# SwitchHead: the small products for the maxima half a turn later, in a turn of scores, value projection, output projection, values

## The reference, cut to what matters

```python
def _moe_attn(x, Wq, Wk, Wv, Wo, Wsel_v, Wsel_o):      # 16 heads of 64, 8 experts, the best 2 kept
    q = _rope(jnp.einsum('bsd,hdp->bhsp', x, Wq))
    k = _rope(jnp.einsum('bsd,hdp->bhsp', x, Wk))
    gv = _gate(x, Wsel_v)
    v = jnp.einsum('bsd,bhse,hedp->bhsp', x, gv, Wv)
    att = jax.nn.softmax(jnp.einsum('bhsp,bhtp->bhst', q, k) / np.sqrt(P), axis=-1)
    o = jnp.einsum('bhst,bhtp->bhsp', att, v)
    go = _gate(x, Wsel_o)
    return jnp.einsum('bhsp,bhse,hepd->bsd', o, go, Wo)
```

## Time and profile before

| | before |
|---|---|
| median of 3 runs | 5247.22 us (5242.2 to 5261.81) |
| the profiled execution's own time | 5249.07 us |
| its span, first to last instruction | 5247.3 us |
| mean granted TensorE clock | 0.956 |
| busy: TensorE, vector engine, ScalarE, GpSimd | 86%, 76%, 63%, 56% of the span |

### The profile page before, as it was taken

One profiled execution on the slowest core, in us unless ns is written; L12 is line 12 of the kernel. 1 busy time (PEld: TensorE's weight loads), 2 busy tenths in 40 slices (PEclk: granted clock), 3 DMA queues, 4 the chain that ended last, 5 costly groups with the idle time before them and its releaser, 6 DMA issues.

```text
span 5247.3 us, 113107 instructions
## 1 busy us (share of the span) xinstructions
PE 4487.2 (86%) x42666; PEld 2217.8 (42%) x42666; DVE 3972.3 (76%) x4717; ACT 3322.4 (63%) x7061; POOL 2912.4 (56%) x2205
## 2 busy tenths in 40 slices
PE   6999998668999999998999888996898888888856
PEld 2333433334555555555555445553333322222226
DVE  5989898768877786778877886776777688888721
ACT  5666565347677777776767666772555557667743
POOL 4888888757867776767767656763212222120014
PEclk8999999889999999999999999998999999999978
DMA  4555555413343343333333332333111111011005
GB/s 149 188 185 181 181 187 189 152 46 97 97 106 93 93 108 88 95 98 89 108 85 92 89 102 74 91 106 72 44 37 31 42 35 23 20 31 20 2 32 170
DMA packets 258831, 488.61 MB, mean 93 GB/s; under 512 B 58731, under 2 KB 108398, under 8 KB 257636
## 3 DMA queue, kind: packets, MB, share of 16 engines
q1 hardware_dynamic: 255288, 475.05, 32.3%
q0 software_dynamic: 3008, 6.32, 0.3%
HBM read 435.33 MB, written 35.30 MB: 90 GB/s over the span
## 4 chain that ended last, share of the span: by engine, by line
PE 65%; issue 13%; DVE 9%; ACT 8%; POOL 5%; DMA 0%; SPq 0%; POOLq 0%; DVEq 0%; ACTq 0%
PE ps L2347 8%; PE ps L1450 8%; PE ps L1440 8%; PE ps L1398 7%; PE ps L1412 7%; PE ps L548 4%; PE ps L2318 4%; PE ps L2300 3%; ACT n_P L2382 3%; PE ps L495 2%; PE ps L1391 2%; DVE ps L713 1%; DVE n_MX L2461 1%; DVE m_HH L734 1%; DVE m_HH L728 1%
## 5 line engine op out<-in xcount | busy, mean ns | idle before, releaser
L2461 DVE TENSOR_REDUCE n_MX<-ps 128x2 f32<-128x1024 f32 (+6 forms) x1034 | 982.4, 979 | 235.8 <-PE ps L2300 134.8
L2382 ACT ACTIVATE n_P<-ps 128x1024 f32<-128x1024 f32 (+4 forms) x1022 | 825.2, 838 | 447.1 <-PE ps L2318 233.5
L1570 ACT ACTIVATE s_P<-s_P,s_MB 128x256 f32<-128x256 f32 x2048 | 1009.5, 501 | 0.3
L1724 DVE TENSOR_REDUCE s_MX<-s_P 128x4 f32<-128x1024 f32 x512 | 599.7, 1213 | 307.8 <-ACT s_P L1555 307.8
L1555 ACT ACTIVATE s_P<-ps 128x1024 f32<-128x1024 f32 x512 | 495.9, 1021 | 380.0 <-PE ps L1412 379.8
L771 POOL TENSOR_TENSOR m_PR<-m_HH,m_CS 128x1024 f32<-128x1024 f32 x256 | 606.0, 2382 | 156.6 <-issue 129.2
L1971 POOL TENSOR_TENSOR XTB<-XTB 128x512 f32<-128x512 f32 x256 | 331.8, 1296 | 586.8 <-DVE XTB L1715 586.8
L1741 DVE STREAM_TRANSPOSE shared<-s_P 128x1024 f32<-128x1024 f32 x512 | 603.2, 1207 | 23.2 <-ACT s_P L1570 23.2
L1952 POOL TENSOR_TENSOR s_OG<-s_OG,s_OT 128x1024 f32<-128x1024 f32 x256 | 606.9, 2372 | 23.7 <-DMA s_OG<-s_gt 23.7
L1450 PE MATMUL ps<-s_OG,s_WO 128*128 128x512 f32 x1024 | 511.9, 623 | 33.6 <-POOL s_OG L1952 23.7
L1412 PE MATMUL ps<-s_QF 64*32 64x256 f32 x16384 | 508.3, 383 | 29.8 <-POOL s_QF L1944 20.0
(11 more groups left out here) (359 smaller groups left out, 6818.4 us busy)
## 6 DMA issues: line engine op xcount, KB each, us to landing
m_CS<-m_rows_c SPq DMA_DIRECT2D x256, 512.0 KB, 3.8
s_OG<-s_gt SPq DMA_DIRECT2D x512, 256.0 KB, 4.2
m_BS<-m_rows_c SPq DMA_DIRECT2D x80, 512.0 KB
s_WV<-in_s_v SPq DMA_DIRECT2D x32, 512.0 KB, 4.0
s_TA<-XTB SPq DMA_DIRECT2D x256, 64.0 KB, 2.3
s_OR<-s_sums SPq DMA_DIRECT2D x128, 128.0 KB, 3.8
s_WO<-in_s_o SPq DMA_DIRECT2D x32, 512.0 KB, 5.3
g_WB<-in_g_wx SPq DMA_DIRECT2D x23, 578.0 KB, 4.3
```

What stands on the lines that cost most here:

```text
L1570: ins = s.activation(P, P, ACT.Exp, bias=self.MB[:, g % 2, 4 * h + a:4 * h + a + 1], accum_out=self.SU[:, g // 4 % 2, at:at + 1])
L2382: ins = s.activation(P[:, at:at + x.shape[1], lo:512], x[:, :, lo:512], ACT.Exp, scale=scale)
L2461: ins = v.tensor_reduce(self.MX[:, q, at:at + x.shape[1], hp, t], x[:, :, 0:width], AX.X, ALU.max)
```

## The change

The join leaves the ring. The flipped maxima and the spread bias get places of their own in the values' bank: self.O shrinks from 512 to 128 columns, self.flip and self.spread lie behind it. So the bank holds one tile's values, keep copies each tile by itself (four copies of 128 columns in place of one of 512), and values wait for the copy of the tile before and for the bias to have been read. In a turn the steps stand in another order: most of tile m-1 and keep of tile m-3 come with the next scores, v comes ahead of gated, onto and max, join comes behind values, and the turn's second transpose behind join.

```diff
-        self.O, self.Z = PS[:, 3072:3584], PS[:, 3584:4096]
-        ring = ("rows", "gate", "gate_t", "qk", "v", "row", "join", "f_t", "f_rows",
+        self.O, self.Z = PS[:, 3072:3200], PS[:, 3584:4096]
+        self.flip, self.spread = PS[0:32, 3200:3328], PS[:, 3328:3336]
+        ring = ("rows", "gate", "gate_t", "qk", "v", "row", "f_t", "f_rows",
...
         k, half = m % 4, lambda late: self.of_half((m - late) // 4)
+        if due(1):
+            out.insert(len(out) - due(0), ("most", *tile(1)))
+        if due(3):
+            out.insert(len(out) - due(0), ("keep", *tile(3)))
...
+        for _ in range(2 if m == 2 else 1):
+            next(vs, None)
         if due(self.GATED):
             h, e = part(self.GATED)
             out.append(("gated", *self.of_half(h), e))
...
         if due(0):
             out.append(("max", *tile(0)))
-        for _ in range(2 if m == 2 else 1):
-            next(vs, None)
-        if due(0):
-            out.append(("join", *tile(0)))
         if due(1):
             out.extend([("exp", *tile(1), 0), ("exp", *tile(1), 1)])
...
         if due(1):
-            out.extend([("turn", *tile(1), 0), ("turn", *tile(1), 1)])
+            out.append(("turn", *tile(1), 0))
...
             out.append(("values", *self.pair(g // 8), g % 8))
-            if g % 4 == 3:
-                out.append(("keep", *self.of_half(g // 4)))
         if due(0):
-            out.append(("most", *tile(0)))
+            out.append(("join", *tile(0)))
+        if due(1):
+            out.append(("turn", *tile(1), 1))
...
             elif kind == "most":
-                g, join = self.tile(*step[1:]), ("join", *step[1:])
+                g = self.tile(*step[1:])
                 pe.wait_ge(self.most_done, g + 1)
+                if g > 0:
+                    pe.wait_ge(self.bias_read, g)
...
-                if g % 4 == 0:
-                    pe.wait_ge(self.o_done, g // 4)
+                if g > 0:
+                    pe.wait_ge(self.o_done, g)
+                pe.wait_ge(self.bias_read, min(g + 2, 64 * NB))
...
             elif kind == "keep":
-                k = self.half(*step[1:])
-                s.wait_ge(self.values_done, 4 * (k + 1))
-                if k > 1:
-                    s.wait_ge(self.ot_done, k - 1)
-                s.activation(self.OR[k % 2][:, 0, :], self.O, ACT.Copy).then_inc(self.o_done, 1)
+                g = self.tile(*step[1:])
+                s.wait_ge(self.values_done, g + 1)
+                if g >= 8:
+                    s.wait_ge(self.ot_done, g // 4 - 1)
+                s.activation(self.OR[g // 4 % 2][:, 0, 128 * (g % 4):128 * (g % 4) + 128], self.O,
+                             ACT.Copy).then_inc(self.o_done, 1)
```

More of the change, by code:

```diff
@@ L898, in __init__ @@
         for name in ("consts_in", "zeroed", "ln_chain", "ln_out", "top_v", "own_top", "b2_done", "spill_out", "top_done", "gates_out", "gv_out", "raw_done", "swap_in", "turn_done",
-                     "rope_done", "wq_in", "wv_in", "gvj_in", "v_done", "mx_zero", "mx_done", "flipped", "most_done", "exp_done",
+                     "rope_done", "wq_in", "wv_in", "gvj_in", "v_done", "mx_zero", "mx_done", "flipped", "most_done", "bias_full", "bias_read", "exp_done",
                      "pt_done", "values_done", "o_done", "su_out", "su_in", "recip_done", "sums_out", "or_in", "ot_done", "og_done", "wo_in", "onto_done", "outt_done", "wf_in", "xn_in", "aff_done",
@@ L933, in order @@
             elif t == 6:
-                out.extend([("most", *self.of_tile(1)), ("turn", *self.of_tile(0), 1)])
+                out.append(("turn", *self.of_tile(0), 1))
         out.append(("gates_of", *self.pair(1)))
@@ L1419, in tensor @@
                 pe.wait_ge(self.mx_done, g + 1)
-                r.empty(pe, step)
-                pe.transpose(ps[0:32, 0:128], self.MX[:, g % 2, :], c.ident[:, :]).then_inc(self.flipped, 1)
+                pe.transpose(self.flip, self.MX[:, g % 2, :], c.ident[:, :]).then_inc(self.flipped, 1)
             elif kind == "most":
-                g, join = self.tile(*step[1:]), ("join", *step[1:])
+                g = self.tile(*step[1:])
                 pe.wait_ge(self.most_done, g + 1)
+                if g > 0:
+                    pe.wait_ge(self.bias_read, g)
                 for x in range(4):
-                    ins = pe.matmul(r.ap(join)[32 * x:32 * x + 32, 512:520], self.MR[:, g % 2, :], c.ident[:, 0:8],
+                    ins = pe.matmul(self.spread[32 * x:32 * x + 32, :], self.MR[:, g % 2, :], c.ident[:, 0:8],
                                     start=True, stop=True)
-                ins.then_inc(*r.fill(join))
+                ins.then_inc(self.bias_full, 1)
             elif kind == "values":
@@ L1433, in tensor @@
                     pe.wait_ge(self.v_done, 8 * (self.turns(b, j) + 1))
-                if g % 4 == 0:
-                    pe.wait_ge(self.o_done, g // 4)
+                if g > 0:
+                    pe.wait_ge(self.o_done, g)
+                pe.wait_ge(self.bias_read, min(g + 2, 64 * NB))
                 for i in range(NT):
                     for h in range(2):
-                        place = self.O[64 * h:64 * h + 64, 128 * (g % 4):128 * (g % 4) + 128].rearrange("p (a n) -> p a n", n=32)
+                        place = self.O[64 * h:64 * h + 64, :].rearrange("p (a n) -> p a n", n=32)
                         P = self.PT[g % 2][:, h, :].rearrange("p (a k n) -> p a k n", a=4, n=32)[:, :, i, :]
@@ L1556, in scalar @@
             elif kind == "most":
-                g, join = self.tile(*step[1:]), ("join", *step[1:])
-                r.filled(s, join)
+                g = self.tile(*step[1:])
+                s.wait_ge(self.bias_full, g + 1)
                 if g > 1:
                     s.wait_ge(self.exp_done, 2 * (g - 1))
-                s.activation(self.MB[:, g % 2, :], r.ap(join)[:, 512:520], ACT.Copy).then_inc(*r.take(join))
+                s.activation(self.MB[:, g % 2, :], self.spread, ACT.Copy).then_inc(self.bias_read, 1)
             elif kind == "exp":
@@ L1564, in scalar @@
                 if h == 0:
-                    r.taken(s, ("join", *step[1:4]))
+                    s.wait_ge(self.bias_read, g + 1)
                     if g % 4 == 0 and g >= 8:
@@ L1730, in vector @@
                 if g > 1:
-                    r.filled(v, ("join", *self.of_tile(g - 2)))
-                v.tensor_reduce(self.MR[0:8, g % 2, :], ps[0:8, 0:128].rearrange("p (x n) -> p n x", x=4), AX.X, ALU.max,
+                    v.wait_ge(self.bias_full, g - 1)
+                v.tensor_reduce(self.MR[0:8, g % 2, :], self.flip[0:8, :].rearrange("p (x n) -> p n x", x=4), AX.X, ALU.max,
                                 negate=True).then_inc(self.most_done, 1)
@@ L1978, in gpsimd @@
                 g.wait_ge(self.or_in, 32 * (k + 1))
-                g.wait_ge(self.o_done, k + 1)
+                g.wait_ge(self.o_done, 4 * (k + 1))
                 if k > 1:
```

## The result

The changed kernel takes 5324.97 us (median of 4 runs, 5319.61 to 5329.88), the kernel before 5247.35 us (4 runs): a ratio of 1.0143, 95% interval 1.0121 to 1.0166. It is slower, by 78 us.

A forecast was written before the change was run, and what follows sets the result against it. TensorE was taken to bound the stage, busy 2231.9 of 2480 us, so only its idle time could change. Terms 64 + 45 + 30 + 5 - 35 - 10 = +99 us on 5249.07 gave 5348 us, range 5275 to 5415.

The forecast's parts named there:

- what comes back: TensorE waits that shrink: flips in the last seven turns or late through ScalarE, s_OUTT, small reduce, vector pieces: -35 us.
- the slot of the key projection: The earlier value projection must wait until the vector engine has read the query or key projection's ring slot: +30 us.
- The turn m%8=1: After each eighth, v waits for values with the maxima and flip queued behind: 3.9 us gap for 1.74, 30 times, +64.
- v's own wait: Sign to look for: in turns m%8=1 the vector engine waits some 3.8 us for the values, about 115 in all.
- The clock: Each of the 30 new gaps ahead of the flip drops TensorE's clock to half and is paid twice: +45 us.
- The rival by which the gap is paid once: Rival, chance 0.15: the clock doesn't fall behind the m%8=1 gaps, so only the gaps count: 5303 us.
- The plain case: Value projection behind a query or key projection, no other work ahead of the slot's read: 0.44 us, 62 turns, 27.
- GpSimd and ScalarE: GpSimd's v steps delay its gate product, +5 us; ScalarE's four small keep copies are hidden, 0.
- vector pieces: Vector engine pieces such as L1660 stand later, about when GpSimd's gate product ends, and run faster: -10 us.
- the rival by which the pieces get out of each other's way: Rival, chance 0.09: all 90 us of TensorE idle time from vector pieces goes, not 10: 5268 us.
- The faster rival: Rival, chance 0.10: TensorE's waits ahead of small products and flip vanish, 170 us less: 5079 us.
- the sentence that the wait could not be met earlier: Against the faster case: values of m-2 can't end 3.6 us earlier for v at m%8=1, as three blocks stand ahead.

The follow-up runs named there:

- wait_off: The changed kernel without the vector engine's own wait for the values at the first v of a pair: 5193.94 us, 0.9882 of the kernel before.
- filler: The changed kernel with nine unread matmuls ahead of the flip in turns m%8=1, filling TensorE's gap: 5286.86 us, 1.0061 of the kernel before.
- v_behind: The changed kernel's late flip and small products, but v behind output projection and maxima as before: 5135.89 us, 0.9772 of the kernel before.
- v_ahead_only: The kernel before with v ahead of gate product, output projection and maxima, and no vector-engine wait for the values: 5691.91 us, ratio 1.0848.

## Why the prediction was right, point by point

The idle times make up the sum: +46.0 (flip), -52.0 (small products), +42.1 (value projection), -1.1 (output projection), +4.2 (scores, 8.2 to 12.4 us), together 39. Busy time adds the other 39: an estimate is 46 by the clock (the difference to wait_off, which has the same order), less 7 that the order saves. That is the 77 us of the turns. The forecast was 99. The mechanism held, and the 21 us too many are in the sizes of two terms: what comes back was put 33 us too small, and the slot of the key projection 12 too small.

*The turn m%8=1.* Forecast: a gap of 3.9 us in place of 1.74 by the same measure, +64 us. Measured: 3.84 us ahead of the flip where 1.68 us stood ahead of the small products, 30 times: +65. One sign came out otherwise: v's own wait was put at 3.8 us each, 115 in all, and measured some 5.1, 154.1 in all. The vector engine reaches v sooner; the gap doesn't grow by that, since v starts when the values end. Taking the wait away moved the time by what was expected, so the cause is shown.

*The clock.* Forecast +45, measured by the filler 38 net, and 45 to 46 in TensorE's busy time. The rule of the Trainium skill ("TensorE: Matmul & The Clock Gate", section "Why this matters for your kernels": idle gaps in mid-kernel bring the clock down to half) agrees: the window behind the gap has a granted clock of 0.59, the one behind the filler 1.00. The rival by which the gap is paid once fell.

*The slot of the key projection.* Forecast +30, measured +42. The plain case was 0.41 us for 0.44 forecast; 20 turns with a piece of other work ahead of L1708 waited 1.4 to 2.5 us, where I had taken 13 turns at 1 us.

*GpSimd and ScalarE.* Forecast +5 and 0; measured +2.4 for gate products and 5.0 ("issue") ahead of the output projection. The 256 small copies of keep cost ScalarE 72.5 us of busy time, 283 ns each, and no wait of TensorE is put down to them.

*What comes back.* This term was mis-sized: -35, and -10 for vector pieces. Outside m%8=1 the idle time ahead of the flip fell by 52 us, in the last seven turns by another 12 (a turn there takes 6.09 us and not 7.93), in m%8=1 the 6.4 that stood there before went, and ahead of s_OUTT 7: some 78 in all. What I had missed is how far the flip's later place helps: I had counted it for the last turns and for ScalarE's late copies, and for the pieces hardly at all. In m%8 = 2, 4, 6 and 7 the flip waited 84.2 us before, 39.4 after, and in v_behind, which has the late flip and v where it was, 36.3. So the late flip alone takes more than half of these waits away; v's earlier place adds nothing. The slow clock in m%8=2 plays a small part: where it stays up, 3.3 us (wait_off) or 3.7 (filler) are left there, for 0.0. The reason I had given for pieces, that they would overlap less with GpSimd, is not borne out: L1660's 56 instructions took 63.5 us before and 62.9 after. So the rival by which the pieces get out of each other's way had half of its size (52 of 90 us) for another reason.

*The faster rival.* Its mechanism was sound for what it named: the small products' wait vanished (54.0 to 2.0), and with v behind the maxima the flip's fell by 90. It lost on the ground given, v's place, in m%8=1. But the sentence that the wait could not be met earlier was too short-sighted: it need not be there at all, and without it the same order is faster than before (0.9882).

## What to carry to other kernels

When a step is moved ahead in an engine's queue, list its waits for every iteration, also for the one in eight that waits for more, and ask what now stands behind that wait and who waits for it. A wait that guards another engine's write is best put on that engine: here one needless wait cost 70 us in the old order and 131 in the new. And a change made of two moves is worth timing in its parts: late flips alone gave 0.9772, v ahead alone (without the wait) 1.0848, and together they gave 1.0143 with the wait and 0.9882 without it.

## What the runs showed of the hardware that I had not expected

Gaps of 1.68 us, one in eight turns, left TensorE's clock alone in the kernel before, all 30 times. With gaps of 1.90 us in most turns it fell behind a third of them: in the windows view of v_ahead_only the turn above has a granted clock of 1.00 up to its gap and 0.61 behind it, and over the stage the mean was 0.94.

```profile
1700.00:1709.60 9.60, 7.78 (x113) 4.47 (x112) 6.03 (x6) 5.89 (x20) 5.70 (x6) 1.00 0.20 56
1709.60:1713.00 3.40, 3.32 (x33) 2.97 (x33) 2.56 (x3) 0.49 (x3) 2.58 (x2) 0.61 0.54 144
```

The next turn, with the same gap of 1.90 us, had its values at 1.97 us again. Of 211 gaps of 1.75 to 2.1 us ahead of the flip, 205 of them within 0.05 us of 1.90, 75 had the clock at 0.50 behind them and values of over 2.2 us, and the other 136 had values of under 2.0. So a gap's length alone did not tell whether it was paid twice.
